# Storing the ffn half early and adding the layer norm in HBM with an accumulating DMA

## The reference

```python
xn = _layernorm(x, axis=-1)
x = x + _L0_attn_ref(xn, ...) + _L0_ffn_ref(xn, weight, bias)

# _L0_attn_ref: in projection (256 -> 2*512), causal conv of 4 taps, silu, scan h = 0.95*h + x,
#   y = h * (s_C B^T) * silu(z), out projection (512 -> 256), then
resid = xn + y
return (resid - mu) * lax.rsqrt(var + LN_EPS) * ln_g + ln_b      # a second layer norm, scaled
# _L0_ffn_ref: xn and weight rounded to a 6-bit grid in blocks of 32, out = xd @ wd.T + bias
```

## Time and profile before

| what | value |
|---|---|
| time, median of 3 runs | 272.79 us (272.72 to 274.57) |
| span of the profiled execution, first to last instruction | 272.2 us |
| the profiled execution's own time | not given beside its span |
| DVE busy | 236.1 us, 353 instructions |
| PE busy | 217.7 us, 1252 matmuls |
| GpSimd busy | 198.4 us, 127 instructions |
| ACT busy | 157.8 us, 240 instructions |
| HBM read and written | 6.76 MB, 4.19 MB |

### The profile page before, as it was taken

How to read it: one execution, slowest core, us unless ns; L and a number is a source line. 1 busy time by engine, 2 the same in 40 slices (tenths; PEclk the granted TensorE clock), 3 DMA queues, 4 the chain that set the end, 5 groups by cost and what they waited for, 6 DMA issues and landing times.

```text
span 272.2 us, 3762 instructions
## 1 busy us (share of the span) xinstructions
PE 217.7 (80%) x1252; PEld 180.9 (66%) x1252; DVE 236.1 (87%) x353; ACT 157.8 (58%) x240; POOL 198.4 (73%) x127
## 2 busy tenths in 40 slices
PE   0469959789999997786999895896999988459940
PEld 0348836467898965775898763785989667359930
DVE  4799999989998999689699999689999978785374
ACT  2797773567953456858755355759737263733540
POOL 1428999999568788986586979985697959943142
PEclk9999995979999999999799999999999999959995
DMA  7963000000000000013202000000202000001204
GB/s 234 291 189 125 1 2 0 1 0 0 2 0 1 2 0 1 2 37 117 78 2 77 0 0 0 0 0 0 77 0 77 2 0 0 0 17 64 77 0 154
DMA packets 10773, 11.12 MB, mean 41 GB/s; under 512 B 648, under 2 KB 10120, under 8 KB 10760
## 3 DMA queue, kind: packets, MB, share of 16 engines
q1 hardware_dynamic: 9488, 9.96, 11.1%
q10 hardware_dynamic: 1272, 0.99, 1.3%
HBM read 6.76 MB, written 4.19 MB: 40 GB/s over the span
## 4 chain that ended last, share of the span: by engine, by line
DVE 32%; PE 31%; issue 16%; ACT 11%; POOL 5%; DMA 2%; DVEq 1%; ACTq 0%; POOLq 0%; SPq 0%
DVE hy L1015 6%; DVE xc L986 4%; DVE nmu L1060 4%; PE slot L747 4%; PE slot L749 4%; PE slot L748 4%; PE obank L839 3%; PE obank L838 3%; PE obank L846 3%; DVE hy L1028 3%; POOL hy L407 2%; ACT xn L586 2%; PE obank L749 2%; PE obank L747 2%; PE obank L748 2%
## 5 line engine op out<-in xcount | busy, mean ns | idle before, releaser
L747 PE MATMUL slot<-xn_hi,w_in_lo 128*128 128x512 f32 x128 | 54.9, 429 | 10.2 <-DVE xd_lo L981 4.1
L399 POOL TENSOR_TENSOR xc<-xc,tap 128x1021 f32<-128x1021 f32 x16 | 46.2, 2887 | 14.9 <-DVE xc L986 14.9
L407 POOL TENSOR_TENSOR hy<-hy,sz 128x1024 f32<-128x1024 f32 x16 | 49.6, 3099 | 6.5 <-ACT sz L630 6.5
L749 PE MATMUL slot<-xn_hi,w_in_hi 128*128 128x512 f32 x128 | 53.2, 416 | 0.0
L748 PE MATMUL slot<-xn_lo,w_in_hi 128*128 128x512 f32 x128 | 53.2, 416 | 0.0
L1015 DVE TENSOR_TENSOR_SCAN hy<-decay,xc 128x1024 f32<-128x1024 f32 x16 | 44.0, 2756 | 0.0
L986 DVE SCALAR_TENSOR_TENSOR xc<-slot,cw,xc 128x1023 f32<-128x1023 f32 (+1 forms) x32 | 40.2, 1264 | 2.3 <-ACT tap L623 1.8
L747 PEld LDWEIGHTS slot<-xn_hi,w_in_lo 128*128 128x128 f32 x128 | 25.7, 201 | 21.5 <-DVE xd_lo L981 5.2
L839 PE MATMUL obank<-w_out_hi,y_hi 128*128 128x256 f32 x128 | 32.8, 287 | 0.0
L838 PE MATMUL obank<-w_out_lo,y_hi 128*128 128x256 f32 x128 | 32.6, 285 | 0.0
L749 PEld LDWEIGHTS slot<-xn_hi,w_in_hi 128*128 128x128 f32 x128 | 25.7, 200 | 6.4
(11 more groups left out here) (109 smaller groups left out, 543.0 us busy)
## 6 DMA issues: line engine op xcount, KB each, us to landing
y<-fx SPq DMA_DIRECT2D x7, 512.0 KB, 2.9
x_in<-L_attn_x SPq DMA_DIRECT2D x3, 1024.0 KB, 5.6
x_in<-L_attn_x SPq DMA_DIRECT2D x2, 512.0 KB, 4.1
rs<-L_attn_W_in SPq DMA_DIRECT2D x2, 512.0 KB, 8.9
fx<-L_attn_W_out SPq DMA_DIRECT2D x1, 512.0 KB, 11.7
y<-fx SPq DMA_DIRECT2D x2, 256.0 KB, 2.1
fx<-L_ffn_weight ACTq DMA_DIRECT2D x1, 256.0 KB, 6.8
xc<-L_attn_B_log ACTq DMA_DIRECT2D x1, 256.0 KB
```

The source lines that it names most:

```text
L399: pool.tensor_tensor(xc[:, c, TAPS - 1:], xc[:, c, TAPS - 1:], tap0[:, c % 2, 0:n], ALU.add).then_inc(conv_ready, 1)
L407: pool.tensor_tensor(hy[:, c, :], hy[:, c, :], sz[:, :], ALU.mult).then_inc(hsz_ready, 1)
L747: pe.matmul(dst, w_lo, m_hi, start=first, stop=False)
L749: return pe.matmul(dst, w_hi, m_hi, start=False, stop=last)
```

## The change

For batches 0 to 2 DVE's finish is gone. SP stores the ffn half as soon as its four tiles are taken (obank_free instead of out_ready). GpSimd gets a new step, add_rs: after its own scale_g and after that store has landed, it issues a DMA that reads rs and adds it to the output in HBM. take(b, 0) and take(b, 4) now also wait until the add that read this half of rs has landed (added[g]). Two small DMAs at the start (the marks) bring both counters of added to 16. The last batch is left as it was, with its out_ready count now 1. At the end SP also waits for the adds.

```diff
+        add_mark = sb("add_mark", [P, 2])
+        added = [sem(f"added{i}") for i in range(2)]
...
             def store(b, g):
 
-                sp.wait_ge(out_ready, 2 * b + g + 1)
+                if is_last(b):
+                    sp.wait_ge(out_ready, 1)
+                else:
+                    sp.wait_ge(obank_free, 2 + NT * b + HT * (g + 1))
                 sp.dma_start(out[b, half(g), :].rearrange("(t p) d -> p t d", p=P),
                              fx[:, tiles(g), :]).then_inc(stored[g], 16)
...
+            for g in range(2):
+                sp.wait_ge(added[g], 16 * (LAST + 1))
             sp.wait_ge(stored[0], 16 * (NB + 1))
...
             pool.wait_ge(const_ready, 2)
+            for g in range(2):
+                pool.dma_start(add_mark[:, g:g + 1], minus_half[:, g:g + 1]).then_inc(added[g], 16)
...
+            @of_batch
+            def add_rs(b, g):
+
+                if not is_last(b):
+                    wait(pool, scaled_ready, 2 * b + g + 1)
+                    wait(pool, stored[g], 16 * (b + 2))
+                    pool.dma_start(out[b, half(g), :].rearrange("(t p) d -> p t d", p=P), rs[:, tiles(g), :],
+                                   accum_op=ALU.add).then_inc(added[g], 16)
...
                 dequantise(here, 1)
+                add_rs(prev, 0)
...
                 conv_tap0(nxt, 1)
                 if first(nxt):
                     w_out_low()
+                add_rs(prev, 1)
                 gate(nxt, 0)
...
                     wait(dve, stored[t // HT], 16 * (b + 1))
+                    wait(dve, added[t // HT], 16 * (b + 1))
                 wait(dve, o_ready, NT * b + t + 1)
...
-            @of_batch
-            def finish(b, g):
-
-                if not is_last(b):
-                    finish_half(b, g)
...
                 y_low(here, 3)
-                finish(prev, 0)
                 block_inverse(nxt, 0)
...
                 take_tile(here, 1)
-                finish(prev, 1)
```

## The result

The changed kernel takes 284.45 us (median of 4 runs, 283.53 to 284.73), the kernel before, timed beside it, 273.53 us (4 runs): ratio 1.038, 95% interval 1.034 to 1.042. The forecast was 272.6 us, its range ended at 277.2. The change costs 10.9 us where it was expected to cost nothing, so the prediction was wrong. The profiled execution grew from 272.2 to 283.0 us.

The account below looks back on a forecast made before the run. No engine bounds it throughout (chain: DVE 32%, PE 31%). +1.45 (step 1) + 0.25 (step 2) - 0.2 (2 to 3) - 1.7 (last) = -0.2 on the 272.2 span: 272.0; median 0.6 above: 272.6 us, range 269.2 to 277.2.

Parts of the forecast that it names:

- Last step: DVE's y_lo runs beside GpSimd's issue in 1.2 instead of 3.16 us, PE's last series starts earlier: -1.7 us.
- Step 2: Issue ahead of the three y_lo starts them 0.25 us late: +0.25; bound: nmu's earlier turn gains up to 1.5 us.
- Step 1: Add waits for the early store queued behind batch 3's load, y_lo late: PE +1.0, clock +1.6, less 1.1: +1.45 us.
- the lead at the taps: In step 1 DVE, without half 1's addition, is 1.1 us early at the taps, taken off the 2.6 us loss.
- Half 1: Removing DVE's half 1 additions gains 1.1 us in step 1, 0.2 in the next, nothing in step 3.
- Issue, marks, landing: GpSimd's issue 1.3 us each; marks at the start free up to 2.5; add lands in 6.3 us without loss.
- Rival B: Slower: the last add lands late, take(3,4) and PE's tile 6 wait; at 10 us landing 277.1 us; chance 0.17.
- C: Rival, slower by a little: GpSimd's issue takes 4 us, +2.2 us, 275.0 us; chance 0.14.
- Rival A: Faster: in step 1 the early store isn't held by the load, landing at 123.5: -4.4, 268.4 us; chance 0.2.
- Its second sum: Rival A's other route: issue between 1.65 and 2.5 us, no clock fall in step 1: about -3.5, 269.3 us.
- If the issue holds DVE off: Last step's lower case: DVE held off during GpSimd's issue, leaving 0.6 of the 1.7 us gain.
- What would show it: Five profile signs: GpSimd's 8 us wait, PE's wait near 131, nmu 0.2 us, last y_lo 1.2, PE's last series near 240.

Follow-up runs that it names:

- e2: Changed kernel with a 1-element GpSimd instruction and a wait for it between the half 0 add and the three y_lo: 274.51 us, 1.003 of before.
- e4: Changed kernel with SP's two stores of batch 0 issued ahead of the load of batch 3: 282.05 us, 1.025 of before.
- e6: Changed kernel with half 1 put back on VectorE, only half 0 added by GpSimd's DMA: 284.31 us, 1.035 of before.
- e5: Changed kernel with half 0 put back on VectorE, only half 1 added by GpSimd's DMA: 271.81 us, 0.992 of before.
- e8: e5 with batch 2's half 1 back on VectorE as well: 273.12 us, 0.994 of before.
- e9: Changed kernel with the edits of e2 and e4 together, a repeat of an identical run: 268.66 us, 0.980 of before.
- e12: e9 with three 1-element operations instead of one behind the half 0 add: 268.28 us, 0.980 of before.
- e3: Kernel before plus a plain 0.5 KB DMA issued by GpSimd at the half 0 add's place: 275.63 us, 1.008 of before.
- e11: Kernel of e9 with a second 1-element operation and wait behind the half 1 add: 267.93 us, 0.975 of before.

## Why the prediction was wrong

**The step that failed** is in "What is added on GpSimd": "In the last step nothing is idle before y_lo ... but the turn changes", and the like for step 2. I had read the alternation of the earlier trace rows as a rule of the two engines and moved the instructions along it. The rule holds only while GpSimd's instructions are vector instructions. With a row of them right behind a DMA issued by GpSimd, VectorE gets no turn until the row ends. The two terms come out so:

- Last step: -1.7 said. VectorE's y_lo took 6.79 us, not 1.2, and PE's last series started 9.84 us late, of which 2.6 arose in that step, with 1.0 more behind it (the clock was at 0.50 from 249 to 255 us and 0.63 to 258). +3.6 in all. Where the turns are given back (e2) the series starts 1.7 us earlier than before, counted from the cut: about what the term had said.
- Step 2: +0.25 said for y_lo being late, with a bound below for nmu's turn. nmu took 4.41 us: +4.1. With the turns given back (e2) the step is 1.7 us shorter than before, about the "up to 1.5 us" that I had named as the bound; so that mechanism was right where nothing spoils it.

**Step 1**: +1.45 said, +3.4 measured. The mechanism stands: the add waits for the early store, which is behind the load. The wait began and ended where it was said, and e4 takes it away. The size is off. PE waited 5.8 us for y_lo:

```profile
136.45 1.22 PE L866 MATMUL obank<-w_out_hi,y_lo 128*128 128x256 f32 x4 [5.82 <-POOL y_lo L425]
```

It came to y_lo's products 1.8 us later than in the earlier trace rows (134.66), where I had 1.0; the difference is the 0.7 us between the store's landing at 127.3 and the start of the issue at 128.02. Counted from the start of the step, 0.3 us earlier in this kernel, it is 2.1. The low clock that I had feared is in this row too, four matmuls in 1.22 us where the earlier trace rows has 0.64. With the 1.6 us that I gave it the two make 3.7. The term that was mis-sized with it is the 1.1 us that I took off for the lead at the taps: e6, where VectorE keeps half 1's addition, has a step 1 of 63.8 us against 63.6 without it, so the lead was worth 0.2 here. e2, without the missing turns, has the same step 1 (63.8), so they cost nothing there.

**Half 1**: -1.3 said, -2.1 measured (e5), nothing for batch 2's (e8). Right in place. In the profile 1.2 of the 2.2 us of step 1 are left once the clock's share is off, near the 1.1 said; how much of the 2.1 over all executions is clock the runs don't say.

**Issue, marks, landing**: 1.33 us, hidden, 6.0 us. All as taken. Rival B (a late last add) was no part of it. By the fit of the Trainium skill (DMA: Bandwidth & Descriptors, "Anatomy of one DMA") a plain transfer would be an estimated 3.2 us; the adding one took 6.0, near twice that; no run here has a plain one of this size.

**The rivals.** C had the right sign with the wrong cause: a long c. Rival A's price for a store that isn't held (268.4) is close to what e9 and e12 reach, but only with the second cure and by other terms, so that is luck. Its second sum is wrong as it stands: the terms add up to -4.2, not -3.5. And the sum's last line set a span of 272.2 beside a median of 272.79 of other executions: the time is 1.7 to 1.8 us above the span of its own execution (284.73 and 283.0 after), so the profile before was of one of about 274.0. "If the issue holds DVE off" asked the wrong question: the issue doesn't (e2), but the row behind it does, until it ends.

**The signs.** Of the five rows named under "What would show it" three came: GpSimd's wait (9.3 us), PE's wait for y_lo from about 131, nmu of step 1 at 0.16 us. The two of the last step, where the failed step stands, didn't.

**What stays open.** That VectorE gets no turn in a row of GpSimd's vector instructions right behind its DMA, and that a stop of 0.46 us (e3) or a small operation with a wait (e2) heals it, is shown. Why is inferred. The Trainium skill (Perfetto Trace Analysis, "GPSIMD Engine Instruction") says that the engine is 8 processors, each with its own queue of instructions, and ("DMA Instruction — SWDGE (GPSIMD)") that the first two of them write a DMA's descriptors. By that, the other six would run ahead into the next vector instruction, two lag behind, and between one instruction and the next there would never be a moment at which all are off the port that VectorE waits for; a wait on a semaphore would bring them together. The 0.45 us of overlap and the 0.5 us on the one-element operation agree, and so does e2's y_lo that runs beside the issue; no run here looks at single processors, and in e3 no overlap shows in the rows.

## What to carry to other kernels

A DMA that GpSimd issues costs more than its issue: look at what GpSimd does right behind it, and if that is a row of large vector instructions while VectorE has work, put the DMA behind them, or a one-element operation and a wait for it between. Where two engines take turns, read from the trace which instruction gets which turn before you count an instruction as removed: asking for one 0.2 us later cost 2.2 us of PE's time, and step 1 grew by 3.9 in all, with the clock low behind the wait. And look at the busy time of the engine that was meant to gain: VectorE lost six instructions and was as busy as before.

## What the runs showed of the hardware that was not expected

- Behind a GpSimd DMA, even of 0.5 KB, with a row of two or three vector instructions right behind it, VectorE's instructions that need a turn wait for the end of GpSimd's whole row: 4.41, 6.12, 6.79 and 7.12 us, for 128x4 elements in two of these places. In e2, with one small operation and a wait behind the DMA, they take 0.16 to 1.23 us.
- The issue of 512 KB in rows of 1 KB took GpSimd 1.3 to 1.4 us, that of 0.5 KB in 128 pieces 0.57 to 0.76.
- An accumulating DMA of 512 KB into HBM landed 6.0 us after its issue, a store of the same bytes 2.9.
- A pause of 2.06 us on PE was followed by the granted clock at 0.50 in a stretch of 3 us (the kernel before); with a pause of 0.44 (e9) or 0.72 (e12) it stayed at 1.00. With 2.08 us in e5's profile and 2.10 in e3's it stayed high as well, so the pause alone doesn't decide it. Nor do the rows: behind the same 1.83 us of waiting at the same time the clock stayed high in e9 and fell in e11.
